# A decoder block on one NeuronCore: probabilities of two heads transposed together in every second slot, in two PSUM banks, and both halves of a tail's rows in one of the slots between

## What is computed

```
x = layernorm(x + attention(x))             # q, k rotated; softmax over masked scores; wei @ v; @ Wo + bo
x = layernorm(x + wkv(w, u, k=x, v=ctx))    # scan over the 256 rows, one recurrence per channel
x = layernorm(x + ffn(x))                   # x @ W.T + bias, plus two of 16 rank-16 experts per row
```

## Time and profile before

| | us |
|---|---|
| median of 3 runs | 1627.79 (1626.96 to 1629.46) |
| the profiled execution | 1626.13 |
| its span in the trace | 1624.30 |
| PE busy | 1545.0 (95%) |
| DVE busy | 1329.1 (82%) |
| ACT busy | 1115.3 (69%) |
| POOL busy | 1011.6 (62%) |
| first 43 us (pipeline fill): PE busy | 23.17 |
| 160 to 1290 us (attention at full flow): PE busy | 1126.65 of 1130.00 |
| 1345 us to the end (last tails, dense layer): PE busy | 242.54 of 279.30 |

### The profile page before, as it was taken

One profiled execution on the slowest core, in us unless ns is written; L12 is line 12 of the kernel. 1 busy time (PEld: TensorE's weight loads), 2 busy tenths in 40 slices (PEclk: granted clock), 3 DMA queues, 4 the chain that ended last, 5 costly groups with the idle time before them and its releaser, 6 DMA issues.

```text
span 1624.3 us, 32607 instructions
## 1 busy us (share of the span) xinstructions
PE 1545.0 (95%) x10464; PEld 1400.8 (86%) x10464; DVE 1329.1 (82%) x3428; ACT 1115.3 (69%) x2979; POOL 1011.6 (62%) x855
## 2 busy tenths in 40 slices
PE   5899999999999999999999999999999977989997
PEld 4799999999999999999999999999999966768885
DVE  4666688898988898988898989888989885967864
ACT  4778777878787878787878787878787764334332
POOL 3455576666666766667666666676667632735652
PEclk9999999999999999999999999999999998999999
DMA  7766444424442444244424442444244412122211
GB/s 236 232 207 230 135 134 150 140 60 145 154 138 60 147 151 139 60 142 155 140 60 149 148 140 59 142 155 140 60 141 152 147 49 88 53 83 74 78 65 52
DMA packets 83144, 202.60 MB, mean 125 GB/s; under 512 B 11808, under 2 KB 12832, under 8 KB 82976
## 3 DMA queue, kind: packets, MB, share of 16 engines
q1 hardware_dynamic: 82976, 200.53, 39.6%
HBM read 120.80 MB, written 37.75 MB: 98 GB/s over the span
## 4 chain that ended last, share of the span: by engine, by line
PE 76%; DVE 12%; issue 5%; ACT 3%; POOL 2%; DVEq 1%; SPq 1%; DMA 0%; ACTq 0%; POOLq 0%
PE bank L507 23%; PE bank L508 22%; PE bank L509 22%; PE bank L621 5%; PE bank L543 2%; DVE PS L1238 1%; DVE RC L1114 1%; PE bank L604 1%; PE bank L612 1%; PE bank L544 1%; DVE QS L1231 1%; ACT Xh L709 1%; DVE OTl L1154 1%; DVE ED L1249 1%; DVE SW L1302 1%
## 5 line engine op out<-in xcount | busy, mean ns | idle before, releaser
L507 PE MATMUL bank<-Xh,W 128*128 128x256 f32 x1280 | 361.8, 283 | 25.4 <-DVE RC L1114 15.4
L509 PE MATMUL bank<-Xh,W 128*128 128x256 f32 x1280 | 359.5, 281 | 0.0
L508 PE MATMUL bank<-Xl,W 128*128 128x256 f32 x1280 | 359.2, 281 | 0.0
L973 POOL TENSOR_TENSOR Ql<-RC,Qh 128x512 fp32r<-128x512 f32 x128 | 171.3, 1338 | 213.8 <-ACT Qh L709 213.8
L724 ACT ACTIVATE S<-S,NM 128x128 f32<-128x128 f32 (+1 forms) x512 | 228.1, 447 | 77.0 <-DVE NM L1099 76.1
L507 PEld LDWEIGHTS bank<-Xh,W 128*128 128x128 f32 x1280 | 243.9, 191 | 29.4 <-DVE RC L1114 11.2
L509 PEld LDWEIGHTS bank<-Xh,W 128*128 128x128 f32 x1280 | 244.0, 191 | 0.0
L508 PEld LDWEIGHTS bank<-Xl,W 128*128 128x128 f32 x1280 | 243.1, 190 | 0.0
L963 POOL TENSOR_TENSOR SW<-SW,tables 128x512 f32<-128x512 f32 x128 | 168.1, 1313 | 119.8 <-DMA SW<-QB 119.7
L709 ACT ACTIVATE S<-S,RL 128x128 f32<-128x128 f32 (+1 forms) x512 | 203.9, 448 | 48.0 <-DVE RL L1106 46.5
L709 ACT ACTIVATE PTh<-bank 128x384 fp32r<-128x384 f32 x256 | 124.9, 488 | 151.1 <-PE bank L621 150.1
(11 more groups left out here) (152 smaller groups left out, 4406.6 us busy)
## 6 DMA issues: line engine op xcount, KB each, us to landing
W<-kept SPq DMA_DIRECT2D x140, 512.0 KB, 4.4
SW<-QB SPq DMA_DIRECT2D x256, 128.0 KB, 2.3
kept<-W SPq DMA_DIRECT2D x40, 512.0 KB, 4.7
XR<-in_xt SPq DMA_DIRECT2D x16, 512.0 KB, 4.3
XR<-XR SPq DMA_DIRECT2D x64, 128.0 KB, 2.4
RO<-in_xn SPq DMA_DIRECT2D x16, 512.0 KB, 3.9
KVT<-in_ctxt SPq DMA_DIRECT2D x16, 512.0 KB, 4.2
mixed<-RO SPq DMA_DIRECT2D x16, 512.0 KB, 4.0
```

Source lines behind the costliest of these rows:

```text
L507: nc.tensor.matmul(dst, lhs[0], rhs[0], start=first, stop=False)
L508: nc.tensor.matmul(dst, lhs[0], rhs[1], start=False, stop=False)
L509: return nc.tensor.matmul(dst, lhs[1], rhs[0], start=False, stop=last)
L973: gp.tensor_tensor(Q[1][:, :, :], RC[:, i % 2, :, :], Q[0][:, :, :], ALU.subtract).then_inc(q_lo, 1)
```

## The change

`L_T` becomes 6 and counts pairs, `L_PT` becomes 7 and counts pairs. So in every even slot PE transposes two heads, six transposes, the first head into bank 3 and the second into bank 7 (`pt_ps` is now a list of two); in odd slots it transposes no probabilities. The heads of one pair used to be transposed in slots 2i+5 and 2i+6 and are now both transposed at the end of slot 2i+6. ACT copies both and DVE subtracts both in the odd slot 2i+7; before, one in slot 2i+6 and one in 2i+7. `S` gets four buffers, `PT` two. The product with V stays in slot 2i+8.

A tail's rows: both halves of `x1` are transposed at lag 2 and both halves of `y` at lag 16, which are odd slots, half 0 into bank 3 and half 1 into bank 7, and both are read one slot later, which is an even slot. Before, the second half came one slot later in each case. Only tails that reach slot 260 or later keep the old spread, in bank 7 alone. The list of who used a bank last (`TURNS`) is kept for each of the two banks, and `bank_free` waits for the reader of the use before: probabilities, `x1` or `y`. The indices into `S` on ACT and DVE change from `g % 2` to `g % 4` (not shown in the diff), and DVE's `maxima` waits for `turned` of head g-4 where it waited for head g-2. The number of instructions and of bytes is the same.

```diff
-L_S, L_T, L_PT, L_WO = 4, 5, 6, 9
-L_NORM, L_SUM, L_Q, L_PV, L_OT = 5, 2, 3, 8, 9
+L_S, L_NORM, L_WO = 4, 5, 9
+L_SUM, L_Q, L_T, L_PT, L_PV, L_OT = 2, 3, 6, 7, 8, 9
 L_ACC = HEADS - 1 + L_WO + 1
...
 TAIL_AT = [t for i in range(PAIRS) for t in (32 * i + 33, 32 * i + 49)]
-T_TURN, T_COPY = 2, 3
+T_TURN = 2
 T_Y = 16
...
 LAST_SLOT = TAIL_AT[-1] + T_END
+TWO_BANKS = ALL + 4
...
-TURNS = []
+def tail_turns(n, behind=0):
+    turns = []
+    for kind, lag in (("x1", T_TURN), ("y", T_Y)):
+        for tau, at in enumerate(TAIL_AT):
+            for t in range(TT):
+                if n - behind == at + lag + (t if at + lag >= TWO_BANKS else 0):
+                    turns.append((kind, tau, t))
+    return turns
+TURNS = {3: [], 7: []}
 for n in range(LAST_SLOT + 1):
-    for t in range(TT):
-        if tail_of(n, T_TURN + t) is not None:
-            TURNS.append(("x1", tail_of(n, T_TURN + t), t))
-        if tail_of(n, T_Y + t) is not None:
-            TURNS.append(("y", tail_of(n, T_Y + t), t))
+    for kind, tau, t in tail_turns(n):
+        TURNS[3 if t == 0 and TAIL_AT[tau] + (T_TURN if kind == "x1" else T_Y) < TWO_BANKS else 7].append((kind, tau, t))
+    if pair_of(n, L_T) is not None:
+        for t in range(2):
+            TURNS[3 + 4 * t].append(("p", 2 * pair_of(n, L_T) + t, 0))
...
         Q = [sb(f"Q{i}", [P, 2, T], fr) for i in "hl"]
-        S = sb("S", [P, 2, P + T])
+        S = sb("S", [P, 4, P + T])
         NM = sb("NM", [P, 2, TT])
...
         RL = sb("RL", [P, 2, TT])
-        PT = [sb(f"PT{i}", [P, 4, P + T], fr) for i in "hl"]
+        PT = [sb(f"PT{i}", [P, 2, P + T], fr) for i in "hl"]
         OT = [sb(f"OT{i}", [P, 2, 2, T], fr) for i in "hl"]
...
         proj_ps = lambda *unit: bank[UNITS.index(unit) % 2][:, 0:T]
-        s_ps, pt_ps, tail_ps = bank[2], bank[3], bank[7]
+        s_ps = bank[2]
+        pt_ps = [bank[3], bank[7]]
+        turn_ps = lambda kind, k, t: bank[next(at for at in TURNS if (kind, k, t) in TURNS[at])]
         acc_ps = bank[5:7]
...
-            def bank_free(kind, tau, t):
-                at = TURNS.index((kind, tau, t))
+            def bank_free(*turn):
+                uses = next(TURNS[at] for at in TURNS if turn in TURNS[at])
+                at = uses.index(turn)
                 if at > 0:
-                    before, k, tt = TURNS[at - 1]
-                    if before == "x1":
-                        pe.wait_ge(kt_copied, TT * k + tt + 1)
+                    before, k, t = uses[at - 1]
+                    if before == "p":
+                        pe.wait_ge(pt_lo, k + 1)
+                    elif before == "x1":
+                        pe.wait_ge(kt_copied, TT * k + t + 1)
                     else:
-                        pe.wait_ge(x2_sum, TT * k + tt + 1)
+                        pe.wait_ge(x2_sum, TT * k + t + 1)
...
                     vs = [[v[:, par, t, j * HD:(j + 1) * HD] for v in V] for t in range(TT)]
-                    pts = [a[:, 2 * (i % 2):2 * (i % 2) + 2, :] for a in PT]
+                    pts = [a[:, :, :] for a in PT]
                     three(ot_ps[:, :, :], vs[0], [a[:, :, 0:T] for a in pts], True, False)
...
                     last.then_inc(wo_done, 1)
-                for t in range(TT):
-                    tau = tail_of(n, T_TURN + t)
-                    if tau is not None:
+                for kind, tau, t in tail_turns(n):
+                    if kind == "x1":
                         pe.wait_ge(x1_done, tau + 1)
-                        bank_free("x1", tau, t)
+                        bank_free(kind, tau, t)
                         for c in range(KC):
-                            last = nc.tensor.transpose(tail_ps[:, c * P:(c + 1) * P],
+                            last = nc.tensor.transpose(turn_ps(kind, tau, t)[:, c * P:(c + 1) * P],
                                                        RO[:, ro_buf(TAIL_BATCH[tau]), t, c * P:(c + 1) * P], Ident[:, :])
                         last.then_inc(x1_turned, 1)
-                    tau = tail_of(n, T_Y + t)
-                    if tau is not None:
+                    else:
                         pe.wait_ge(y_done, 2 * tau + 2)
-                        bank_free("y", tau, t)
+                        bank_free(kind, tau, t)
                         for c in range(KC):
-                            last = nc.tensor.transpose(tail_ps[:, c * P:(c + 1) * P], EV[:, c, t * P:(t + 1) * P], Ident[:, :])
+                            last = nc.tensor.transpose(turn_ps(kind, tau, t)[:, c * P:(c + 1) * P], EV[:, c, t * P:(t + 1) * P], Ident[:, :])
                         last.then_inc(y_turned, 1)
-                g = head_of(n, L_T)
-                if g is not None:
-                    pe.wait_ge(normed, g + 1)
-                    above(pe, pt_lo, g)
-                    if g == 0:
+                i = pair_of(n, L_T)
+                if i is not None:
+                    if i == 0:
                         pe.wait_ge(const_in, 16 * len(CONSTS))
-                    for k in range(3):
-                        last = nc.tensor.transpose(pt_ps[:, k * P:(k + 1) * P], S[:, g % 2, k * P:(k + 1) * P], Ident[:, :])
-                    last.then_inc(turned, 1)
+                    for g in (2 * i, 2 * i + 1):
+                        pe.wait_ge(normed, g + 1)
+                        bank_free("p", g, 0)
+                        for k in range(3):
+                            last = nc.tensor.transpose(pt_ps[g % 2][:, k * P:(k + 1) * P], S[:, g % 4, k * P:(k + 1) * P], Ident[:, :])
+                        last.then_inc(turned, 1)
...
             def probabilities(n):
-                g = head_of(n, L_PT)
-                if g is not None:
-                    act.wait_ge(turned, g + 1)
-                    above(act, mixed_v, g // 2 - 1)
-                    copy(PT[0][:, g % 4, :], pt_ps[:, 0:P + T]).then_inc(pt_hi, 1)
+                i = pair_of(n, L_PT)
+                if i is not None:
+                    above(act, mixed_v, i)
+                    for g in (2 * i, 2 * i + 1):
+                        act.wait_ge(turned, g + 1)
+                        copy(PT[0][:, g % 2, :], pt_ps[g % 2][:, 0:P + T]).then_inc(pt_hi, 1)
...
                     norm("x2", tau, RS2, NM2, x2_done)
-                for t in range(TT):
-                    tau = at(T_COPY + t, 0)
-                    if tau is not None:
+                for kind, tau, t in tail_turns(n, 1):
+                    if kind == "x1" and place == 0:
                         act.wait_ge(x1_turned, TT * tau + t + 1)
...
                             act.wait_ge(w_lo, HALVES * NP)
-                        copy(KT[:, :, t * P:(t + 1) * P], tail_ps[:, :].rearrange("p (c t) -> p c t", c=KC)).then_inc(kt_copied, 1)
+                        copy(KT[:, :, t * P:(t + 1) * P], turn_ps(kind, tau, t)[:, :].rearrange("p (c t) -> p c t", c=KC)).then_inc(kt_copied, 1)
                 for lag, p, what, h in EXPONENTS:
...
             def probabilities(n):
-                g = head_of(n, L_PT)
-                if g is not None:
-                    dve.wait_ge(pt_hi, g + 1)
-                    v.tensor_tensor(PT[1][:, g % 4, :], pt_ps[:, 0:P + T], PT[0][:, g % 4, :], ALU.subtract).then_inc(pt_lo, 1)
+                i = pair_of(n, L_PT)
+                if i is not None:
+                    for g in (2 * i, 2 * i + 1):
+                        dve.wait_ge(pt_hi, g + 1)
+                        v.tensor_tensor(PT[1][:, g % 2, :], pt_ps[g % 2][:, 0:P + T], PT[0][:, g % 2, :], ALU.subtract).then_inc(pt_lo, 1)
...
                         v.tensor_tensor(two(EV, h), two(EV, h), two(ED, h), ALU.mult).then_inc(y_done, 1)
-                for t in range(TT):
-                    tau = at(T_Y + 1 + t, 0)
-                    if tau is not None:
+                for kind, tau, t in tail_turns(n, 1):
+                    if kind == "y" and place == 0:
                         dve.wait_ge(y_turned, TT * tau + t + 1)
-                        v.tensor_tensor(rows(tau)[:, t, :], tail_ps[:, :], rows(tau)[:, t, :], ALU.add).then_inc(x2_sum, 1)
+                        v.tensor_tensor(rows(tau)[:, t, :], turn_ps(kind, tau, t)[:, :], rows(tau)[:, t, :], ALU.add).then_inc(x2_sum, 1)
                 tau = at(T_END - 2, 1)
...
                     dve.wait_ge(x2_sum, TT * tau + TT)
```

More of the change, by code:

```diff
@@ L720, in exponentials @@
                 if g is not None:
-                    i = g % 2
                     act.wait_ge(maxed, g + 1)
                     for t, c in ((0, slice(0, P)), (1, slice(P, P + T))):
-                        last = nc.scalar.activation(S[:, i, c], S[:, i, c], ACT.Exp, bias=NM[:, i, t:t + 1],
-                                                    scale=-1.0, accum_out=L[:, i, t:t + 1])
+                        last = nc.scalar.activation(S[:, g % 4, c], S[:, g % 4, c], ACT.Exp, bias=NM[:, g % 2, t:t + 1],
+                                                    scale=-1.0, accum_out=L[:, g % 2, t:t + 1])
                     last.then_inc(exped, 1)
```

(12 more changed lines are left out.)

## The result

After takes 1634.8 us (median of 5 runs), before 1627.8; the ratio is 1.0046 with a 95% interval of 1.0031 to 1.0061. The forecast was 1632.2. The profiled execution spans 1631.4 us where before spanned 1624.3, 7.1 more.

The account below looks back on a forecast made before the run. PE was taken to bound the kernel, busy 1126.65 of 1130.00 us from 160 to 1290 us. Terms 2.0 + 1.7 + 0.8 + 1.0 - 0.9 - 0.2 = +4.4 on 1627.8 gave 1632.2 us; 8-in-10 range 1625.5 to 1638.5.

Parts of the forecast that it names:

- PE's own work: PE's transposes and matmuls: no price for switching to transposes, taken as 0, bounds zero and -2.6 us; work moves 0.33 us.
- Lag 10 of every second tail: PE waits behind DVE's scans: five slots 0.39 us later (+2.0), two like slot 139 0.85 later (+1.7).
- Lag 10 of the other tails: Six slots, 59 to 219: DVE already late, of ACT's 0.39 us only 0.13 is left each, +0.8 us.
- rival B: Slower, 1636.3, chance 0.18: even-slot relief lost; six other tails get 0.47, not 0.13 (+2.0); margins at lags 7, 15 fail (+2.1).
- Lag 8: Seven slots, 57 to 249: scan and Ql come 0.35 us late, scores wait 0.05 to 0.15; +1.0 us (0 to 2).
- Lag 6: Slots 103, 135 and 199: PE's waits go, because DVE enters odd slots 0.47 us earlier; -0.9 us.
- The bank at lag 17: PE's wait for L1260, 0.17 us booked, stays, as the probabilities now need both banks; no change in time.
- The ends: After 1298 us -0.5 and +0.3 us; fill of the first 160 us 0, with 2 us both ways; together -0.2.
- The signs named in advance: ACT's idle below half of 151 us; L1114 waits 5 to 8 us, nearly all lag 11; slot 139's QS about 2 us.
- C: Turns with POOL do not follow the shift, DVE alone counts: +3.0 us, 1630.8, called no change; chance 0.12.
- A: Faster: ACT's new slack in even slots lets late engines catch up, ending PE's waits at lag 10; 1622.9, chance 0.10.

Follow-up runs that it names:

- The last experiment: After with the second subtraction behind QS at lag 10, a 384-byte unused tile, and DVE's two sums at lag 17 ahead of the norm-shift instruction: 1621.9 us, ratio 0.9963.
- the short subtraction: After, with the second subtraction covering 128 of 384 columns in the odd slot at lag 10 of each tail: 1632.7 us, ratio 1.0032 to before.
- the delayed DVE: Before, plus a DVE statistics instruction over 384 columns ahead of QS at lag 10 of thirteen tails: 1632.0 us, ratio 1.0028.

## Why the prediction was near, step by step

**PE's own work, priced at zero: right within its bounds.** The median odd slot is 4.89 us long where it was 5.13, the median even one 5.03 for 4.80: a shift of 0.23 to 0.24, where 0.33 was expected. The pair of slots 14 and 15 of each 32, where PE never waits, takes 9.80 us before and 9.84 after (medians of seven; 9.80 to 9.89 after). It did not become shorter, so it shows no price of the switch. The -1.5 us left over from slot 36 on lies within the bound of -2.6, but moving a tile moves the same sum by as much and more (160.7 to 162.0 us for 32 slots), so it says nothing of the switches.

**Lag 10 of every second tail, +3.7: right in sum (+3.8)**, and by its mechanism. The five measured 0.43 to 0.54 each for 0.39. Slot 139 measured 0.92 for 0.85. Slot 203, forecast at 0.85, took the other order, because POOL happened to be late there, and lost 0.3 at the next scores: without that luck this term would have been too small.

**Lag 10 of the other tails, +0.8: too small, +1.7.** I took them to be late by themselves, so that the even slot's relief would pay for most. It did, but below it lies the chain of the odd slot alone, `Qh`, `Ql`, 1.09, `PS`, which is the same for all tails and gives 0.78. This is half of rival B's first step. I should have computed that floor instead of correcting the old lateness.

**Lag 8, +1.0: too large, +0.6.** **Lag 6, -0.9: right, -0.7**; the waits named went, and slot 247 got one of 0.4, since its projection waits for L1131 again.

**The bank at lag 17, zero: wrong, +1.2.** I wrote that the wait for L1260 stays. It grew, since the probabilities of the pair need both banks and the second sum comes 0.6 us behind the first. PE in slot 66 of after; the six transposes, which start 0.11 apart elsewhere, take 0.87 from the first start to the scores:

```profile
354.92 0.39 PE L524 MATMUL bank<-W,OTl 128*128 128x512 f32 x1
355.38 1.11 PE L638 MATMUL bank<-Ident,S 128*128 128x128 f32 x6
356.25 0.36 PE L561 MATMUL bank<-KHL,Qh 128*128 128x256 f32 x1
```

The view of waits no longer lists it: each part is too short. The last experiment, which moved the sums and lost these waits, shows the cause.

**Not in the sum: slot 226, +0.9.** There the norm statistics, 0.47 later behind the second subtraction, meet a POOL operation, and a 2-column DVE instruction takes 0.97 us; the same instruction takes 0.17 in slot 66, ahead of POOL's next operation.

```profile
1167.34 1.29 POOL L970 TENSOR_TENSOR Xl<-XR,Xh 128x512 fp32r<-128x512 f32 x1 [2.54 <-ACT Xh L726]
...
1167.68 0.97 DVE L1195 TENSOR_SCALAR VE<-MV 128x2 f32<-128x2 f32 x1 [0.26 <-issue]
...
1169.15 0.39 PE L522 MATMUL bank<-Xh,W 128*128 128x256 f32 x1 [0.67 <-DVE RC L1131]
```

I had gone through the odd slots up to their own end and not to what they hand to the next. **The ends, -0.2: +1.1 in this execution**, where the clock was lower.

**The sum: +4.4 forecast, +7.1 in the trace and +7.0 at the medians.** The two terms put at nothing or left out (the banks at lag 17 and slot 226) make +2.1 of the difference, the ends +1.3, the other tails +0.9, lag 6 +0.2 and lag 10 of every second tail +0.1; against them stand -1.5 of PE's own work and -0.4 at lag 8. That the forecast is not further off is in part luck, for the -1.5 was not foreseen.

**The signs named in advance.** ACT's idle time ahead of the copies fell below half, `QS` in slot 139 takes 2.02 us behind `Ql`, and 12 of 14 waits stand at lag 11, as said. The waits for L1114 (now L1131) were to be 5 to 8 us and are 8.4.

**The choice between the rivals.** C (DVE's shift alone counts) fell with the short subtraction and with the delayed DVE. A's hope, that ACT's slack helps, came to nothing: of the 90 us less ahead of the copies ACT spends 76 more in waiting for `RL`, and PE waited more. B (1636.3) is nearer to the measured 1634.8 than the forecast is. Half of its first step is in the other tails, as said; its second, waits at lags 7 and 15, did not come. So what slowed the kernel beyond the forecast was mostly not B's mechanism.

## What to carry to other kernels

Where two engines exclude each other for whole instructions, ask of each meeting who starts first and by how much; a lead of 0.04 us decided over a microsecond here, and an edit elsewhere can flip it either way. Put the long, critical one ahead by the order of its own engine's instructions, not by a wait on the other. And before a change of 0.3% is credited to its idea, compare the pitch of the instructions that nobody touched.

## What was not expected of the hardware

An unused tile of 24 bytes a partition lengthened the distance of the 256-column matmuls in odd slots from 115.7 to 117.3 ns, one of 384 bytes shortened it to 114.9, and the kernel's time moved by +0.12% and -0.17%. Added work on ACT (two copies, 0.27 us) removed five waits of PE, and lengthened six.
